# Two scans over interleaved columns in the recurrence of a GRU kernel

## The reference, cut to what matters

```python
x = x + attention_block(x, cond, ...)           # x: [16, 256, 512]; 16 heads of 32; runs first
x = x + gru(cond, x, W_ih, W_hh, b_ih, b_hh)    # 256 time steps, one after the other

def cell(h, x):                                  # h: [16, 512]
    gi = x @ W_ih + b_ih                         # [16, 1536]
    gh = h @ W_hh + b_hh
    i_r, i_z, i_n = split(gi); h_r, h_z, h_n = split(gh)
    r = sigmoid(i_r + h_r)
    z = sigmoid(i_z + h_z)
    n = tanh(i_n + r * h_n)
    return (1 - z) * n + z * h                   # the new h, also this step's output
```

## Time and profile before

| what | value |
|---|---|
| median of 3 runs | 1676.29 us (1675.59 to 1678.32) |
| the profiled execution's own time | 1676.52 us |
| its span, first to last instruction | 1674.7 us |
| PE busy | 1658.6 us, 99% of the span |
| DVE busy | 1194.5 us, 71% |
| ACT busy | 933.4 us, 56% |
| POOL busy | 409.3 us, 24% |
| granted TensorE clock | 1.0 of full speed throughout |

### The profile page before, as it was taken

The page is one execution under the profiler, slowest core; times in us unless marked ns, Lnnn a source line. Parts: engine busy times, 40 slices in busy tenths (PEclk is TensorE's granted clock), DMA queues, the critical chain, the costliest instruction groups (busy, mean ns, idle before and its releaser), DMA issues.

```text
span 1674.7 us, 71812 instructions
## 1 busy us (share of the span) xinstructions
PE 1658.6 (99%) x30549; PEld 1292.1 (77%) x30549; DVE 1194.5 (71%) x4267; ACT 933.4 (56%) x3139; POOL 409.3 (24%) x464
## 2 busy tenths in 40 slices
PE   9999999999999999999999999999999999999998
PEld 7787777888788887777777777777777777777776
DVE  6888878888888876666666666666666666666665
ACT  5777777777777776444444444444444444444443
POOL 4544444444444430011111111111111111111111
PEclk9999999999999999999999999999999999999999
DMA  6244443333344426211111111111111111111110
GB/s 202 57 118 124 115 100 89 89 96 96 96 97 102 94 76 149 44 30 25 31 30 27 28 30 27 30 29 27 32 28 27 32 29 26 32 29 26 31 25 16
DMA packets 234280, 100.02 MB, mean 60 GB/s; under 512 B 141196, under 2 KB 213720, under 8 KB 233960
## 3 DMA queue, kind: packets, MB, share of 16 engines
q1 hardware_dynamic: 233840, 95.40, 23.0%
q10 hardware_dynamic: 120, 0.04, 0.0%
HBM read 58.38 MB, written 36.96 MB: 57 GB/s over the span
## 4 chain that ended last, share of the span: by engine, by line
PE 95%; DVE 1%; ACT 1%; POOL 1%; SPq 1%; issue 1%; DMA 1%; DVEq 0%; ACTq 0%; POOLq 0%
PE ps L763 40%; PE ps L649 20%; PE ps L512 14%; PE ps L591 7%; PE ps L627 5%; PE ps L572 4%; PE ps L606 3%; PE ps L614 1%; POOL rq L1431 1%; SPq L285 0%; PE ps L551 0%; ACT P L1237 0%; PE ps L533 0%; DVE nmx L872 0%; PE ps L541 0%
## 5 line engine op out<-in xcount | busy, mean ns | idle before, releaser
L649 PE MATMUL ps<-wih,x1T 128*32 128x192 f32 x8192 | 379.6, 326 | 0.3 <-issue 0.3
L1373 ACT ACTIVATE v<-ps 128x128 f32<-128x128 f32 x512 | 140.7, 275 | 414.6 <-PE ps L763 414.6
L763 PE MATMUL ps<-whh,hTE 128*32 128x192 f32 x8192 | 356.3, 326 | 1.1 <-DVE hTE L1102 1.1
L763 PE MATMUL ps<-whh,hTO 128*32 128x192 f32 x8192 | 356.3, 326 | 0.0
L1486 POOL TENSOR_TENSOR outG<-hG,x1g 128x128 f32<-128x128 f32 x255 | 116.3, 456 | 920.4 <-DVE hG L1095 920.4
L649 PEld LDWEIGHTS ps<-wih,x1T 128*32 128x32 f32 x8192 | 266.5, 110 | 66.7 <-issue 0.6
L763 PEld LDWEIGHTS ps<-whh,hTE 128*32 128x32 f32 x8192 | 249.8, 110 | 84.3 <-DVE hTE L1102 15.5
L763 PEld LDWEIGHTS ps<-whh,hTO 128*32 128x32 f32 x8192 | 250.0, 110 | 83.0 <-issue 0.4
L1075 DVE SCALAR_TENSOR_TENSOR v<-v,ps 128x64 f32<-128x64 f32 x512 | 113.4, 222 | 237.5 <-ACT v L1373 237.5
L1237 ACT ACTIVATE P<-ps,nmx 128x256 f32<-128x256 f32 x496 | 229.7, 483 | 0.3 <-DVE nmx L872 0.3
L1381 ACT ACTIVATE v<-v 128x64 f32<-128x64 f32 x512 | 131.5, 257 | 132.5 <-DVE v L1080 132.5
(11 more groups left out here) (139 smaller groups left out, 2155.5 us busy)
## 6 DMA issues: line engine op xcount, KB each, us to landing
xres<-in_x_dram SPq DMA_DIRECT2D x32, 256.0 KB, 3.4
xscr<-x1s SPq DMA_DIRECT2D x32, 256.0 KB, 2.5
xblk<-x1s SPq DMA_DIRECT2D x128, 64.0 KB, 2.7
x1g<-xscr SPq DMA_DIRECT2D x128, 64.0 KB, 2.0
out_dram<-outG SPq DMA_DIRECT2D x252, 32.0 KB, 1.7
x1n<-xblk SPq DMA_DIRECT2D x124, 64.0 KB, 1.9
kscr<-xt SPq DMA_DIRECT2D x30, 256.0 KB, 2.0
xt<-kscr SPq DMA_DIRECT2D x60, 128.0 KB, 2.8
```

The source lines that it names most:

```text
L649: last = pe.matmul(gb[pr % 2][q][32 * j:32 * j + 32, 64:256], x1T[:, tt % 2, r, c, :], wig[:, c, :, 128 * j + 64 * q:128 * j + 64 * q + 64 ...
L763: last = pe.matmul(gb[e][q][32 * j:32 * j + 32, 0:192], h[:, c, :], whg[:, c, :, 128 * j + 64 * q:128 * j + 64 * q + 64], start=False, sto ...
L1373: s.activation(v_rz[:, q, :], gb[e][q][:, 64:192], ACT.Tanh, scale=0.5).then_inc(s_tr, 1)
```

## The change

The gates of a bank now lie in columns 0 to 383, six columns for each of the 64 features: h_n, r, z, i_n, and two unused. So h_n and i_n of one feature are three columns apart, and a read with a step of three columns takes h_n, i_n, h_n, i_n and so on. Both kinds of matmul write with a step of six columns inside a block of 64.

`before_n` is one VectorE scan over 128 columns: it multiplies the running value by data0 and adds data1. data0 is 0, r, 0, r, ...; data1 is h_n, i_n, h_n, i_n, ...; so every odd column ends as r * h_n + i_n. `new_h` is a second scan with data0 = 0, 1-z, 0, 1-z, ... and data1 = n, z*h, n, z*h, ...; every odd column ends as n * (1-z) + z * h. `r_times_n` and `new_part` are gone, each for both halves, that is four VectorE operations in a step. `z_times_h` is a plain product. ScalarE uses Sigmoid for the gates, and writes r, z, 1-z and n to every second column of tiles of which the other columns are cleared once by GpSimd (`rz2`, `c2`); the new h, too, is every second column of `h2`. TensorE gets four matmuls of 384 columns with the identity before the first `x_group`, which mark the gate columns of banks 0 to 3 as written; the first seeds wait for these (`s_mk`).

```diff
-        gb = [[ps[:, 2 * e + q, 256:512] for q in range(2)] for e in range(2)]
+        gb = [[ps[:, 2 * e + q, 0:384].rearrange("p (k s) -> p s k", s=6) for q in range(2)] for e in range(2)]
+        both = [[ps[:, 2 * e + q, 0:384:3] for q in range(2)] for e in range(2)]
...
-                    last = pe.matmul(gb[pr % 2][q][32 * j:32 * j + 32, 64:256], x1T[:, tt % 2, r, c, :],
+                    last = pe.matmul(gb[pr % 2][q][32 * j:32 * j + 32, 1:4, :], x1T[:, tt % 2, r, c, :],
...
+            for bank in range(4):
+                last = pe.matmul(ps[:, bank, 0:384], ident, ident.unsqueeze(1).to_broadcast([128, 3, 128]), start=True, stop=True)
+            last.then_inc(s_mk, 1)
...
-                        last = pe.matmul(gb[e][q][32 * j:32 * j + 32, 0:192], h[:, c, :],
+                        last = pe.matmul(gb[e][q][32 * j:32 * j + 32, 0:3, :], h[:, c, :],
...
-                def r_times_n(q):
+                def before_n(q):
+
                     v.wait_ge(s_tr, 2 * t + q + 1)
-                    v.scalar_tensor_tensor(out=v_v[:, q, :], in0=v_rz[:, q, 0:64], scalar=1.0, in1=gb[e][q][:, 0:64],
-                                           op0=ALU.add, op1=ALU.mult).then_inc(s_u, 1)
-
-                def before_n(q):
-                    v.wait_ge(s_u, 2 * t + q + 1)
-                    v.scalar_tensor_tensor(out=v_w[:, q, :], in0=v_v[:, q, :], scalar=0.5, in1=gb[e][q][:, 192:256],
-                                           op0=ALU.mult, op1=ALU.add).then_inc(s_w, 1)
+                    v.tensor_tensor_scan(out=n_in[:, q].rearrange("p k a -> p (k a)"), data0=rz2[:, q, 0].rearrange("p k a -> p (k a)"),
+                                         data1=both[e][q], initial=0.0,
+                                         op0=ALU.mult, op1=ALU.add).then_inc(s_w, 1)
...
-                    v.scalar_tensor_tensor(out=v_h[:, q, :], in0=v_rz[:, q, 64:128], scalar=1.0, in1=h_old[:, f[q]],
-                                           op0=ALU.add, op1=ALU.mult)
-
-                def new_part(q):
-
+                    v.tensor_tensor(n_zh[:, q, :, 1], rz2[:, q, 1, :, 1], h_old[:, f[q]], ALU.mult).then_inc(s_d, 1)
+
+                def new_h(q):
+
+                    v.wait_ge(s_d, 2 * t + q + 1)
                     v.wait_ge(s_n, 2 * t + q + 1)
-                    v.tensor_tensor(v_n[:, q, :], v_n[:, q, :], v_c[:, q, :], ALU.mult).then_inc(s_d, 1)
-
-                def new_h(q):
-                    v.wait_ge(s_d, 2 * t + q + 1)
-                    v.scalar_tensor_tensor(out=h_new[:, f[q]], in0=v_h[:, q, :], scalar=0.5, in1=v_n[:, q, :],
-                                           op0=ALU.mult, op1=ALU.add).then_inc(s_h, 1)
+                    v.tensor_tensor_scan(out=h_new[:, f[q], :].rearrange("p k a -> p (k a)"), data0=c2[:, q].rearrange("p k a -> p (k a)"),
+                                         data1=n_zh[:, q].rearrange("p k a -> p (k a)"), initial=0.0,
+                                         op0=ALU.mult, op1=ALU.add).then_inc(s_h, 1)
...
                     if t < T - 1:
                         v.wait_ge(s_h, 2 * t + q + 1)
                         v.transpose(turned(t)[:, 2 * q:2 * q + 2, :],
-                                    h_new[:, f[q]].rearrange("p (c k) -> p c k", c=2)).then_inc(s_hc, 1)
+                                    h_new[:, f[q], 1].rearrange("p (c k) -> p c k", c=2)).then_inc(s_hc, 1)
...
-                r_times_n(0)
                 before_n(0)
                 if t >= 2:
                     v.wait_ge(s_og, t - 1)
                 z_times_h(0)
-                new_part(0)
-                r_times_n(1)
                 new_h(0)
                 before_n(1)
                 turn_h(0)
                 z_times_h(1)
-                new_part(1)
                 new_h(1)
...
-                s.copy(ps[:, 2 * e:2 * e + 2, 256:512].rearrange("p q (g f) -> p q g f", g=4),
+                s.copy(ps[:, 2 * e:2 * e + 2, 0:384].rearrange("p q (k s) -> p q s k", s=6)[:, :, 0:4, :],
                        Bc.rearrange("p g (q f) -> p q g f", q=2)).then_inc(s_sd, 1)
 
             s.wait_ge(s_bias, 1)
-            s.wait_ge(s_S, NP)
+            s.wait_ge(s_mk, 1)
             seed(0)
             seed(1)
 
+            s.wait_ge(s_z0, 2)
...
-                    s.activation(v_rz[:, q, :], gb[e][q][:, 64:192], ACT.Tanh, scale=0.5).then_inc(s_tr, 1)
+                    s.activation(rz2[:, q, :, :, 1], gb[e][q][:, 1:3, :], ACT.Sigmoid).then_inc(s_tr, 1)
...
-                    s.activation(v_c[:, q, :], v_rz[:, q, 64:128], ACT.Copy, bias=0.5, scale=-0.5)
+                    s.activation(c2[:, q, :, 1], rz2[:, q, 1, :, 1], ACT.Copy, bias=1.0, scale=-1.0)
...
-                    s.activation(v_n[:, q, :], v_w[:, q, :], ACT.Tanh).then_inc(s_n, 1)
+                    s.activation(n_zh[:, q, :, 0], n_in[:, q, :, 1], ACT.Tanh).then_inc(s_n, 1)
...
+            g_.wait_ge(s_qkv, 6 * NB)
+            g_.memset(rz2, 0.0).then_inc(s_z0, 1)
+            g_.memset(c2, 0.0).then_inc(s_z0, 1)
```

More of the change, by code:

```diff
@@ L184, in cond_resid_kernel @@
         x1n0 = sb("x1n0", [128, D])
+        rz2 = sb("rz2", [128, 2, 2, 64, 2])
+        c2 = sb("c2", [128, 2, 64, 2])
         assert base[0] <= a_wi
@@ L192, in cond_resid_kernel @@
         base[0] = a_P
-        v_rz, v_v, v_w, v_n, v_c, v_h = (sb(f"v{k}", [128, 2, 128 if k == 0 else 64]) for k in range(6))
+        h2 = sb("h2", [128, 2, 128, 2])
+        n_in, n_zh = (sb(n, [128, 2, 64, 2]) for n in ("n_in", "n_zh"))
         base[0] = a_sq
@@ L238, in cond_resid_kernel @@
         s_xb = [sem("x1_blocks_out0"), sem("x1_blocks_out1")]
+        s_z0, s_mk = sem("even_cleared"), sem("gate_columns_marked")
         s_hz, s_b0, s_lwh, s_lwi = (sem(n) for n in ("h_cleared", "h0_load", "whh", "wih"))
@@ L251, in cond_resid_kernel @@
         s_sum = [sem("sum0"), sem("sum1")]
-        s_tr, s_u, s_w, s_n, s_d, s_h, s_hc, s_hs, s_og = (
-            sem(n) for n in ("rz", "rn", "pre_n", "n", "parts_h", "h", "h_turned", "h_shifted", "og"))
+        s_tr, s_w, s_n, s_d, s_h, s_hc, s_hs, s_og = (
+            sem(n) for n in ("rz", "pre_n", "n", "z_h", "h", "h_turned", "h_shifted", "og"))
         def emptied(eng, piece):
@@ L1069, in _ @@
                 e = t // 2 % 2
-                h_old, h_new = hs.rearrange("p c k -> p (c k)"), hG[:, t % 2, :]
+                h_old, h_new = hs.rearrange("p c k -> p (c k)"), h2[:, t % 2]
                 f = [slice(0, 64), slice(64, 128)]
-                def r_times_n(q):
+                def before_n(q):
                     v.wait_ge(s_tr, 2 * t + q + 1)
-                    v.scalar_tensor_tensor(out=v_v[:, q, :], in0=v_rz[:, q, 0:64], scalar=1.0, in1=gb[e][q][:, 0:64],
-                                           op0=ALU.add, op1=ALU.mult).then_inc(s_u, 1)
@@ L1083, in z_times_h @@
                 def z_times_h(q):
                     v.wait_ge(s_hs, t + 1)
-                    v.scalar_tensor_tensor(out=v_h[:, q, :], in0=v_rz[:, q, 64:128], scalar=1.0, in1=h_old[:, f[q]],
-                                           op0=ALU.add, op1=ALU.mult)
-                def new_part(q):
-                    v.wait_ge(s_n, 2 * t + q + 1)
-                    v.tensor_tensor(v_n[:, q, :], v_n[:, q, :], v_c[:, q, :], ALU.mult).then_inc(s_d, 1)
+                    v.tensor_tensor(n_zh[:, q, :, 1], rz2[:, q, 1, :, 1], h_old[:, f[q]], ALU.mult).then_inc(s_d, 1)
@@ L1093, in new_h @@
                 def new_h(q):
                     v.wait_ge(s_d, 2 * t + q + 1)
-                    v.scalar_tensor_tensor(out=h_new[:, f[q]], in0=v_h[:, q, :], scalar=0.5, in1=v_n[:, q, :],
-                                           op0=ALU.mult, op1=ALU.add).then_inc(s_h, 1)
+                    v.wait_ge(s_n, 2 * t + q + 1)
+                    v.tensor_tensor_scan(out=h_new[:, f[q], :].rearrange("p k a -> p (k a)"), data0=c2[:, q].rearrange("p k a -> p (k a)"),
+                                         data1=n_zh[:, q].rearrange("p k a -> p (k a)"), initial=0.0,
+                                         op0=ALU.mult, op1=ALU.add).then_inc(s_h, 1)
@@ L1129, in _ @@
             v.wait_ge(s_h, 2 * T)
-            v.tensor_tensor(outG[:, (NT - 1) % 2, ST - 1, :], hG[:, (T - 1) % 2, :], x1g[(NT - 1) % 2][:, ST // 2 - 1, :],
+            v.tensor_tensor(outG[:, (NT - 1) % 2, ST - 1, :], h2[:, (T - 1) % 2, :, 1], x1g[(NT - 1) % 2][:, ST // 2 - 1, :],
                             ALU.add).then_inc(s_last, 1)
@@ L1485, in _ @@
                         g_.wait_ge(s_out[tt % 2], 128 * (tt // 2))
-                g_.tensor_tensor(outG[:, tt % 2, k, :], hG[:, t % 2, :], x1g[tt % 2][:, k // 2, :],
+                g_.tensor_tensor(outG[:, tt % 2, k, :], h2[:, t % 2, :, 1], x1g[tt % 2][:, k // 2, :],
                                  ALU.add).then_inc(s_og, 1)
```

## The result

The changed kernel takes 1702.23 us (1701.84 to 1702.56, 4 runs), the kernel before 1676.15 us in the same comparison: a ratio of 1.0153 with a 95% interval of 1.0135 to 1.0171. It is 26 us slower. The direction was forecast; the size was not: 1683 had been given, 7 us slower. The time lies in the prediction's range (1677 to 1740), in the region of rival C.

A forecast was written before the change was run, and what follows sets the result against it. TensorE was taken to bound the recurrence at 3.90 us a step, with the other engines' loop 0.02 us shorter. 1676.5 + 3.4 (start) + 3 (loop) = 1683 us; range 1677 to 1740.

The forecast's parts named there:

- rival C: In the recurrence, strided operands or a scan of up to 0.5 us stretch the loop: 1692 to 1743 us; chance 0.25.
- TensorE's floor of 3.90 us and the loop's slack of 0.02 us: In the recurrence TensorE's columns need 3.90 us a step; the loop through the other engines, uncovered, takes 3.88 us.
- The scan: One VectorE scan of 128 columns in the recurrence was estimated at 427 ns, with bounds of 293 and 616 ns.
- The loop after: From gates(0) through the scans, turn_h(0) starts at 1.72 us instead of 1.69, costing +3 us over 254 steps.
- Strided tiles: Column steps in gates(0), tanh_n(0) and turn_h(0) were taken as 0, with bounds of 0 to +57 us.
- The predicted 0.03 us of extra loop: Later start of turn_h(0) in each step; less the slack of 0.02 us, over 254 steps, it costs +3 us.
- Table load: Sigmoid may need another ScalarE load of 1.28 us before the first gates, run early in idle time: 0 us.
- Half 1: The second half's path in a step: turn_h(1) at 2.59 us against about 2.61 before, so not what is late next.
- The start: Four identity matmuls and a seed before x_group(0) delay all later TensorE work by +3.4 us; bounds 2.6 and 3.8.
- rival A: The forecast itself: a scan in the recurrence near 0.43 us, strides free; 1680 to 1692 us; chance 0.42.
- Rival B: A scan at or below 0.42 us stays hidden behind TensorE's 3.90 us; only the start costs: 1679.5 us; chance 0.17.
- Rival D: TensorE writes strided PSUM columns slowly, so a step doubles: +994 us, about 2680 us; chance 0.13.

The follow-up runs named there:

- uncovered run before: The kernel before with six of the eight x_group calls of every pair but the first left out; 1670.1 us.
- one semaphore: The changed kernel with the product z*h adding to tanh's semaphore, so new_h waits for one semaphore instead of two; 1683.53 us.
- other order: The changed kernel with new_h's two waits swapped, first for tanh, then for VectorE's own product; 1683.65 us.
- layout run: The kernel before with only the new PSUM layout, six columns to a feature, no scans or Sigmoid, marks left by the last scores; 1676.05 us.
- Tanh run: The changed kernel with Tanh of half the argument in place of Sigmoid, every access pattern kept; 1700.2 us.

## Why the prediction went wrong in size

- **TensorE's floor of 3.90 us and the loop's slack of 0.02 us**: right. The uncovered run before has 3.880, and a faster loop gains nothing.
- **The scan**: right. 427 ns estimated, 408 (one source in PSUM) and 425 ns measured, at two column times a column. The Trainium skill ("DVE: opcode table, instruction layouts, handler registers and perf-mode slots", section Datapath and trigger behaviour) says that the scan runs at half throughput; the trace agrees, with 2.08 ns a column against the 1.05 of a plain operation.
- **The loop after**: here it failed. The step "scan new_h starts 0.29 after tanh_n(0), as new_part did" carried new_part's distance over to an instruction that waits for two semaphores, where new_part had one. The diff shows both `wait_ge` lines; they were read as one event. Price: 0.07 us a step, 18.7 us. It is shown from two sides in the changed kernel (one semaphore, other order), and the same wait put into the kernel before cost 13.8 us.
- **Strided tiles**: taken as 0 with bounds of 0 to 0.22 us a step. Measured: gates +0.024 (SBUF write, as the layout run and the Tanh run together show), tanh_n and one_less_z +0.011, turn_h -0.010 in the mean. Left over from all of it, once the wait is gone, is 0.008 us a step, 2 us; the sign and the bounds were right. The reason given for 0 did not hold: 0.81 ns a column for ScalarE is about half the pace of an fp32r matmul (0.85 - 0.40 = 0.45 ns), not twice, and it is ScalarE's SBUF side that cost something.
- **The predicted 0.03 us of extra loop** therefore became 0.10 (3.98 against 3.88). In step 254 turn_h(0) starts at 1.79 instead of 1.72: 0.02 of the gates and 0.07 of the wait, less 0.02 from before_n(1), after which the queue is free a little sooner. From turn_h(0) to the matmuls it is 0.27 instead of 0.29, as turn_h(0) takes 0.22 instead of 0.24 us. That gives the 3.96 of the table. The last 0.02 up to the mean is not seen in step 254 and is not traced to an operation; it belongs to the loop, since the run without most of x_group has it too.
- **Table load**: one more, as forecast, but 1.3 us on the path where the sum had 0. Its place was read from an instruction with one wait; the first gates have two (GpSimd's clearing and TensorE's sums), and the load stands between the separate wait, the one for TensorE, and the activation.
- **Half 1**: "not what is late next" held in size only. Its turned h comes late in every step too, but costs next to nothing beside half 0.
- **The start**: 3.4 us forecast, 3.2 measured; with the table load 4.5 by the trace, and 4.9 between the medians when both were taken out.
- **The ranges**: by the prediction's own formula a scan of 435 ns gives 1689 us, not the 1692 at which rival A ends, and the overall range stops at 1740 where C reaches 1743. Neither bears on the result.
- **Rival B** (hidden scan) fell with the scan's 425 ns. **Rival C** named the right region, the loop stretches, for causes that made up a small part of it (strides) or none (the scan); that the time lies in its range is luck. **Rival D** (slow strided writes by TensorE) fell: the layout run measured 326 ns records and a ratio of 1.0. The Trainium skill ("PSUM — Partial Sum Buffer", section Specifications) says that any non-contiguous pattern slows matmuls significantly; for a step of six columns this trace does not agree. The measurement decides, for fp32 matmuls of 192 columns in four column groups; faster formats were not tried.

## What to carry to other kernels

Before two engines trade work in a loop that is nearly as long as the bounding engine's step, find the one step where the bound is absent: it gives the slack, here 0.02 us, and so the price of every hundredth. Count waits as well as instructions: where an operation needs two semaphores, let the late one be the one that rides on the operation (here the wait written first), or let both producers raise one semaphore. And put a first use of a new activation function where ScalarE is idle, since the table load stayed behind a wait that was its own instruction.

## What the runs showed of the hardware that was not expected

- A second wait before a VectorE operation, satisfied long before, delayed the operation by 0.07 us when the separate wait was the one that came last; the order of the two lines in the code decided it (1702.2 against 1683.65 us).
- ScalarE's table load of 1.28 us started only after a separate wait for TensorE, at the end of 7.18 us of idle time; a one-column activation right behind the seeds moved it to 667.36 us, off the path.
- x_group on one column group of TensorE took 1.46 us in 8 records, the same as four groups with 32 records (1.48).
- A ScalarE write to every second fp32 column in SBUF took 299 ns instead of 275 for 128 columns and 268 instead of 257 for 64. A VectorE transpose that reads every second column took 233 ns instead of 243 in the mean: no price seen.
